# Eight-layer transformer kernel: the first mixture's LayerNorm and turns placed inside the first attention's last tiles, and waits of the feature attention changed

## The reference

```python
x = x + _L0_xattn_ref(_layernorm(x, axis=-1), ctx_2048, ...)   # layer 0: quantized attention, 16 heads
x = x + _L0_ffn_ref(_layernorm(x, axis=-1), ...)               # layer 1: first mixture, shared expert
...
x = x + _L2_ffn_ref(_layernorm(x, axis=-1), ...)               # layer 5: second mixture
x = x + _L3_xattn_ref(_layernorm(x, axis=-1), ctx_2048, ctx_2048)  # layer 6: feature attention
x = x + _L3_ffn_ref(_layernorm(x, axis=-1), ...)               # layer 7: keyed experts and an MLP
```

```python
# layer 0, end of the attention
out = _qdq(o) @ _qdq(wp).T + bp
# layer 1, the router
logits = h.astype(jnp.float32) @ gate_weight.astype(jnp.float32).T
scores = jax.nn.softmax(logits, axis=-1)
topk_w, topk_i = _group_limited_topk(scores)
# layer 5, the weighted sum of two experts a token
for e in range(NUM_EXPERTS):
    gate = jax.nn.silu(jnp.einsum('bsd,dh->bsh', x, W1[e]))
    val = jnp.einsum('bsd,dh->bsh', x, W3[e])
    y = jnp.einsum('bsh,hd->bsd', gate * val, W2[e])
    out = out + combine[..., e:e + 1] * y
# layer 6
qk = jnp.einsum('bdm,bdn->bmn', qh, kh) * scale
sm = jax.nn.softmax(qk, axis=-1)
ret = jnp.einsum('bmn,bcn->bcm', sm, vh)
```

## Time and profile before

| | us |
|---|---|
| median of 3 runs | 1147.91 |
| lowest and highest of them | 1144.64 and 1151.24 |
| the profiled execution | 1144.83 |
| its span, first to last instruction | 1143.1 |
| PE busy in it | 1027.7 (90%) |
| DVE busy in it | 574.1 (50%) |
| ACT, POOL busy in it | 367.9 (32%), 260.5 (23%) |
| mean granted clock of TensorE | 0.946 |

### The profile page before, as it was taken

How to read it: one execution, slowest core, us unless ns; L and a number is a source line. 1 busy time by engine, 2 the same in 40 slices (tenths; PEclk the granted TensorE clock), 3 DMA queues, 4 the chain that set the end, 5 groups by cost and what they waited for, 6 DMA issues and landing times.

```text
span 1143.1 us, 17534 instructions
## 1 busy us (share of the span) xinstructions
PE 1027.7 (90%) x6658; PEld 687.7 (60%) x6658; DVE 574.1 (50%) x1312; ACT 367.9 (32%) x687; POOL 260.5 (23%) x335
## 2 busy tenths in 40 slices
PE   5877999989999999988864899999939999998989
PEld 4665599546767676667654677777713434453467
DVE  7985523444334343445476112212166787647792
ACT  3651233232121212213310222212104666736660
POOL 4221342410000000003521222222142443302350
PEclk9995999999999999999895999999966999989999
DMA  9002033211011010056016112111060000020000
GB/s 290 22 2 101 3 95 93 88 47 28 15 37 35 28 38 5 11 200 255 2 57 256 33 35 102 35 33 37 19 232 1 2 1 1 2 74 1 0 6 33
DMA packets 37433, 67.26 MB, mean 59 GB/s; under 512 B 4456, under 2 KB 27080, under 8 KB 35816
## 3 DMA queue, kind: packets, MB, share of 16 engines
q1 hardware_dynamic: 29960, 51.98, 13.3%
q0 software_dynamic: 4080, 11.15, 3.5%
q10 hardware_dynamic: 3312, 3.02, 0.8%
HBM read 54.72 MB, written 11.40 MB: 58 GB/s over the span
## 4 chain that ended last, share of the span: by engine, by line
PE 73%; DVE 16%; ACT 3%; issue 3%; DMA 3%; POOL 2%; SPq 0%; POOLq 0%; DVEq 0%; ACTq 0%
PE bank L354 20%; PE bank L1192 12%; PE bank L1216 7%; PE bank L1542 5%; PE bank L2244 4%; PE bank L2269 3%; PE bank L2290 3%; PE bank L1552 3%; PE bank L1205 2%; PE bank L1527 2%; PE bank L2726 2%; PE bank L1517 2%; PE bank L2308 1%; DVE big L2519 1%; PE bank L1177 1%
## 5 line engine op out<-in xcount | busy, mean ns | idle before, releaser
L1192 PE MATMUL bank<-big 128*128 x552 | 147.7, 417 | 0.6 <-ACT big L1068 0.6
L354 PE MATMUL bank<-XNT,big 128*128 128x512 f32 x296 | 135.9, 607 | 6.4 <-DVE big L2472 3.8
L1192 PEld LDWEIGHTS bank<-big 128*128 128x128 f32 x552 | 98.2, 191 | 39.4 <-issue 2.6
L270 POOL TENSOR_TENSOR rstd<-ve,half 128x1 f32<-128x1 f32 x56 | 32.7, 588 | 340.1 <-DVE ve L264 339.8
L2244 PE MATMUL bank<-big,xs 32*128 32x512 f32 x256 | 88.1, 736 | 19.4 <-DVE xs L281 18.5
L354 PEld LDWEIGHTS bank<-XNT,big 128*128 128x128 f32 x296 | 54.8, 193 | 69.3 <-issue 59.5
L2111 DVE TENSOR_REDUCE big<-bank 128x2 f32<-128x512 f32 x128 | 81.9, 685 | 24.3 <-PE bank L2244 23.7
L1216 PE MATMUL bank<-big 128*128 (+1 forms) x368 | 87.2, 380 | 1.1 <-ACT big L1083 1.1
L1004 DVE TENSOR_TENSOR big<-big,bank 128x704 f32<-128x704 f32 x23 | 20.5, 889 | 124.7 <-ACT big L1076 124.7
L2190 ACT ACTIVATE big<-bank 128x1024 f32<-128x1024 f32 x64 | 64.9, 1024 | 38.6 <-PE bank L2269 38.3
L354 PE MATMUL bank<-CTXT,big 128*128 128x512 f32 (+1 forms) x192 | 67.0, 493 | 10.9 <-DMA big<-wvT 10.9
(11 more groups left out here) (351 smaller groups left out, 1798.5 us busy)
## 6 DMA issues: line engine op xcount, KB each, us to landing
big<-m_gu SPq DMA_DIRECT2D x8, 1408.0 KB
big<-m_d SPq DMA_DIRECT2D x8, 768.0 KB
big<-a_qk SPq DMA_DIRECT2D x16, 256.0 KB, 3.0
yg<-big ACTq DMA_DIRECT2D x23, 128.0 KB
big<-m_gu SPq DMA_DIRECT2D x8, 352.0 KB
big<-a_o SPq DMA_DIRECT2D x16, 128.0 KB, 2.1
xn<-XNT SPq DMA_DIRECT2D x8, 256.0 KB, 5.9
big<-f_keys SPq DMA_DIRECT2D x1, 2048.0 KB, 9.1
```

Source lines behind the costliest of these rows:

```text
L270: e.tensor_tensor(k.rstd[at % NT][:, :], k.ve[at % NT][:, :], k.half[:, 0:1], ALU.pow).then_inc(k.ln_rstd, 1)
L354: ins = e.matmul(out, a, b, start=start and n == 0, stop=stop and n == len(pairs) - 1)
L1192: ins = e.matmul(out, xgT[s % 2][:, kb, :], WB[:, bass.ds(at[s] + (kb * 2 * F + c * chunk), chunk)], start=kb == 0, stop=kb == KB - 1)
```

## The change

**First mixture.** `experts` lends stage 0 five functions (`stats`, `norm`, `turn`, `logits`, `rows`), and stage 0 issues them among its last steps. DVE makes the statistics of tiles 0 to 3 between `outputs(6)` and `result(6)`, normalises 0 to 2 ahead of `outputs(7)` and 3 behind it, makes the statistics of 4 to 6 ahead of `result(7)`, and the rest behind it; the clears come last. POOL makes its powers for tiles 0 to 3, 4 to 6 and 7 in three instructions in place of eight. PE turns tiles 0 to 2 and makes the logits of 0 and 1 around `out_rows(7)` and `result(7)`; the other turns and logits follow. `XN` moves behind `sg` and `sh` in SBUF, and with it the second attention's `XS`; `TURN` becomes banks 1 and 5, which stage 0 no longer uses by then.

```diff
@@ attention_qdq, dve
+            if front and i == NT - 1:
+                for t in range(4):
+                    front["stats"](e, t)
             if i > 0:
                 result(i - 1)
...
+        if front:
+            for t in range(3):
+                front["norm"](e, t)
         outputs(NT - 1)
+        if front:
+            front["norm"](e, 3)
+            for t in range(4, 7):
+                front["stats"](e, t)
         result(NT - 1)
+        if front:
+            front["stats"](e, 7)
+            for t in range(4, NT):
+                front["norm"](e, t)
@@ attention_qdq, act
+        if front:
+            front["rows"](e, 0)
+            front["rows"](e, 1)
         out_rows(NT - 1)
+        if front:
+            front["rows"](e, 2)
@@ attention_qdq, pe
+        if front:
+            front["turn"](e, 0)
+            front["turn"](e, 1)
+            front["logits"](e, 0)
         out_rows(NT - 1)
+        if front:
+            front["turn"](e, 2)
         result(NT - 1)
+        if front:
+            front["logits"](e, 1)
@@ experts
+    def front_stats(e, t):
+
+        e.wait_ge(k.x_tile, done0 - NT + t + 1)
+        ln_stats_dve(e, k, k.chain(e, "dve"), t, t % 2)
...
+    ahead = 3 if shared_expert and l >= 1 else 0
+    if ahead:
+        k.front[1] = dict(stats=front_stats, norm=norm_x, turn=turn_x, logits=logits, rows=rows_in)
+
+    def pool_first(e):
+        if ahead:
+            ln_rstd_tiles_pool(e, k, at0, 0, 4)
+            ln_rstd_tiles_pool(e, k, at0, 4, 7)
+            ln_rstd_tiles_pool(e, k, at0, 7, 8)
```

```diff
@@ experts, dve
-        for t in range(NT):
+        def combine(t):
...
+        if not shared_expert and k.front.get(6):
+            k.front[6]["combine"] = combine
+            return
+        for t in range(NT):
+            combine(t)
@@ feature_attention
+    if l >= 6:
+        k.front[6] = {}
+    y_ps, y_all = k.moe["y_ps"], k.moe_at["y_ps"]
+
+    def ready(e):
+
+        e.wait_ge(y_ps, y_all)
...
+        def x_of(t):
+
+            if k.front.get(6):
+                k.front[6]["combine"](t)
+                e.wait_ge(k.x_tile, done0 - NT + t + 1)
+
         e.wait_ge(k.masks, masks0 + 2)
+        x_of(0)
         ln_stats_dve(e, k, ch, 0, 0)
+        x_of(1)
         norm(0)
...
+        x_of(2)
+        x_of(3)
         for u in range(NU):
@@ program, run
-                if n > 1 and who != "sp":
-
+                if "ready" in s and who != "sp":
+                    s["ready"](e)
+                elif n > 1 and who != "sp":
                     e.wait_ge(k.x_tile, LOADED + 8 * (n - 1))
```

More of the change, by code:

```diff
@@ L487, in result @@
             e.tensor_tensor(k.X[:, t, :], k.X[:, t, :], k.bank[:, V, D:2 * D], ALU.add).then_inc(k.x_tile, 1)
+        front = k.front.get(1)
         e.wait_ge(k.x_first, 16)
@@ L865, in pool @@
     def pool(e):
-        for t in range(NT):
+        for t in range(0 if ahead else NT):
             ln_rstd_pool(e, k, at0 + t, t % 2)
@@ L910, in dve @@
         ch = k.chain(e, "dve")
-        for t in (0, 1):
-            ln_stats_dve(e, k, ch, t, t)
+        if not ahead:
+            for t in (0, 1):
+                ln_stats_dve(e, k, ch, t, t)
         for n in range(4):
@@ L915, in dve @@
             ch.mark(e.memset(sums[n][:, 0:E], 0.0))
[L916 to L920, removed]
+        for t in range(0 if ahead else NT):
+            norm_x(e, t)
             if t + 2 < NT:
-                ln_stats_dve(e, k, ch, t + 2, p)
+                ln_stats_dve(e, k, ch, t + 2, t % 2)
         lg = k.bank[:, LOGIT, 0:NT * E].rearrange("p (t e) -> p t e", e=E)
@@ L1040, in dve, with rows_in, turn_x, logits @@
                     k.front[2]["norm"](e, n)
-    def act(e):
[L1043 to L1048, removed]
+    def rows_in(e, t):
+        e.wait_ge(k.xt_ps, at0 + t + 1 + CREDIT)
+        dst = k.XNT[:, :, t * P:(t + 1) * P] if shared_expert else k.xT[t % 2][:, :, :]
+        if not shared_expert and t >= 2:
+            after(e, "lg_ps", t - 1)
+        e.copy(dst, k.bank[:, TURN[t % 2], 0:D].rearrange("p (k m) -> p k m", k=KB)).then_inc(k.xt_sb, 1)
+    def turn_x(e, t):
+        e.wait_ge(k.ln_out, at0 + t + 1)
+        e.wait_ge(k.xt_sb, at0 + t + 1)
+        for kb in range(KB):
+            ins = e.transpose(k.bank[:, TURN[t % 2], kb * P:(kb + 1) * P], XN[:, t, kb * P:(kb + 1) * P], k.ident[:, :])
+        ins.then_inc(k.xt_ps, 1)
+    def logits(e, t):
+        if t == 0:
+            after(e, "gate_ld", ends["gate_ld"])
+        e.wait_ge(k.xt_sb, at0 + t + 1 + CREDIT)
+        xT = k.XNT[:, :, t * P:(t + 1) * P] if shared_expert else k.xT[t % 2]
+        tell(mm(e, k.bank[:, LOGIT, t * E:(t + 1) * E], [(xT[:, kb], gw[:, kb]) for kb in range(KB)]), "lg_ps")
+    def front_stats(e, t):
+        e.wait_ge(k.x_tile, done0 - NT + t + 1)
+        ln_stats_dve(e, k, k.chain(e, "dve"), t, t % 2)
+    def norm_x(e, t):
+        e.wait_ge(k.ln_rstd, at0 + t + 1)
+        e.tensor_scalar(XN[:, t], k.X[:, t, :], k.mv[t][:, 0:1], k.rstd[t][:, 0:1], ALU.subtract, ALU.mult)\
+            .then_inc(k.ln_out, 1)
+    ahead = 3 if shared_expert and l >= 1 else 0
[6 more added lines that the diff above has]
+            ln_rstd_tiles_pool(e, k, at0, 7, 8)
+    def act(e):
+        for t in range(ahead, NT):
+            rows_in(e, t)
         def shared(n):
@@ L1128, in shared_down @@
                     [(sh[0:n, t // 4, b, t % 4 * P:(t % 4 + 1) * P], shd[0:n, b]) for b, n in enumerate(FB)]), "shy_ps")
[L1130 to L1133, removed]
[L1134 to L1139 removed]
+        if not ahead:
+            turn_x(e, 0)
+        for t in range(max(ahead - 1, 0), NT):
             if t + 1 < NT:
[L1141 to L1144 removed]
+                turn_x(e, t + 1)
+            logits(e, t)
         if shared_expert:
@@ L2129, in rest @@
             t, n = divmod(u, UNITS)
+            if half == 1 and u < UNITS:
+                x_of(u + 4)
             if n == 0 and half == 0 and t + 2 < NT:
```

23 lines of the change are left out of this document (8 added, 15 removed).

## The result

| | before | after |
|---|---|---|
| median of 20 runs, us | 1149.80 | 1142.34 |
| lowest and highest | 1144.64 and 1152.60 | 1140.11 and 1145.66 |
| ratio, 95% interval | | 0.9935 (0.9925 to 0.9945) |
| the profiled execution's span | 1143.1 | 1143.8 |

The change makes the kernel 7.5 us faster (6.3 to 8.6), where 6.8 were forecast. The two profiled executions do not show it: their spans are alike. The one of before was among the fastest of its kernel, the one of after, 1145.5 us in all, among the slowest of its own. So no gain is read from the spans; every stretch is measured by itself, between two instructions that both kernels have.

The account below looks back on a forecast made before the run. The last-ending chain, 73% PE and 16% DVE, was taken as the bound, with exposed hops at layer 0's end and layer 6's start. Gains 5.4 + 1.4 = 6.8 us off the median 1147.91 gave 1141.1, range 1135 to 1146.

Parts of the forecast that it names:

- Both: Stretch from start of outputs(6) to start of the routing; the first mixture's logits were forecast to end 5.4 us earlier.
- the Score: Time from start of the last instruction of layer 5's sums to layer 6's first score; forecast 1.4 us shorter.
- DVE ahead of outputs(7): End of layer 0: four statistics, a power and three normalisations make outputs(7) 0.6 us late, bounds 0 to 1.1.
- PE: Turns and logits of first tiles fit gaps, projection ends at 96.41, tile 4 just in time, logits end 5.4 us earlier.
- Part 2: Passage to layer 6: statistics directly behind the last sum, power not behind the keys; 1.4 us, bounds 0.7 to 1.6.
- A: Rival: layer 5's sums do get spread out inside layer 6, first score 8.6 us early, 12.5 us gained; 4%.
- B: Rival: DVE's new work delays the last tile more, handed through without slack; gain only 4.9 us, 1143.0; 22%.
- C: Rival: DVE and POOL block one another, nearest at tile 4's normalisation beside a power; up to 0.66 us, 1141.8; 6%.
- D: Rival: layer 6's new start leads to a low TensorE clock for longer, some 20 us more giving 1151; 4%.
- its counterpart: Rival: TensorE's clock in layer 6 rises some 6 us earlier, giving 3 us more, 1138; 6%.
- a rise of the clock more than 5 us behind the logits' end: Sign of a wrong forecast, gain given back; the expected lag was some 3 to 4 us, as before.
- a stretch after 110 that is longer than before by more than 1 us: Sign of a wrong forecast: the gain was made and then given back later in the kernel.

Follow-up runs that it names:

- three_first: Changed kernel with statistics of three tiles instead of four made first on DVE, tile 3's moved behind outputs(7); ratio to the kernel before 0.9940.
- after_third: The changed kernel itself, unmodified, run and profiled a third time beside other kernels on the same chip; ratio to the kernel before 0.9942.
- after_again: The changed kernel itself, unmodified, run once more for a second profile; ratio to the kernel before 0.9938.
- part2_only: Changed kernel without the functions lent to layer 0, so only layer 6's new wait is left; ratio to the kernel before 0.9997.
- part1_again: Same program as part1_only, traced a second time; no timing given, its trace shows 7.52 us from result(7) to the routing.
- part1_only: Changed kernel with layer 6's new wait taken out, so only the first mixture's part is left; ratio to the kernel before 0.9951.
- sums_deferred: Changed kernel with k.front[6] made true, so later tiles' sums come inside layer 6; ratio to the kernel before 0.9890, 12.6 us faster.

## Why the prediction was right

**Where the gain lies.** Both shrank by 5.52 us for 5.4 forecast, the Score by 1.50 for 1.4. Of the total, 7.5 us in the first comparison, and 7.1 and 6.7 in the two others, 7.0 are these two. The clock's rise in the tail, 1.3 us in 3 of 11 traces, adds some tenths that were not forecast. The time forecast, 1141.1, and the 1142.34 measured differ mostly by the kernel before: its median was 1147.91 in the 3 runs that the forecast rests on and 1149.80 in 20.

**DVE ahead of outputs(7).** Forecast 0.6 us late, measured 0.39. The power began 0.30 behind the last `ve` and took 1.03, as forecast. But the statistics began 0.08 ahead of the end of `outputs(6)`, not 0.03 behind it, and each overlapped the one before as in the rows. DVE starts an independent instruction before the last has ended, which I had allowed for in part 2 and not here.

**PE.** The last projection began at once behind turn 2, and from `result(7)` to the routing it took 7.54 us. Forecast were 103.8 for the logits' end, with the projection's end at 96.4: 7.4. The "just in time" of the forecast missed by a little: DVE had normalised tile 4 by 99.01 + 0.41 = 99.42, and PE began its turn at 99.47, 1.30 behind tile 3's turn at 98.17 where a tile costs 1.17. So 0.13 us were lost there. Turn 2 cost nothing, where 0.06 were forecast: from `out_rows(7)` to the projection it took 1.15 us before and after. With 0.21 less delay of DVE, 0.06 less of turn 2 and some 0.14 more in the tail, the forecast's 5.4 becomes the 5.5 measured.

**Part 2.** That the sums are not spread out was read from the order of the instructions, and the trace bears it out: all 16 sums ahead of the statistics. The two halves of its gain came as forecast: the statistics behind the last sum by 0.41 instead of 1.21, the power no longer behind the keys.

**The rivals.** A did not happen, and its price was right when it was made to: 12.6 us for 12.5. Its terms were nearly so: the first score came 8.6 us earlier behind the first sum (3.45 for 12.06), as forecast, and Tile 0 was 2.3 longer than before, where 1.5 were forecast; the trace had the clock's rise in the tail besides. B's mechanism is real, since each us on DVE is handed through, but its price was too high: 0.39 us of delay for the 1.1 of its bound. C cost nothing where the prediction had placed it: the four normalisations from 99.01 on took 1.37 us, with POOL's power at 99.17 beside them; three without any took 1.06, and a fourth at the same distance gives 1.38. A wait shows on POOL's side, though. The power at 99.17 took 0.65 us, as the 655 ns one of the earlier trace rows, also of one tile, did beside normalisations; in `three_first` one of the same form took 0.54 beside statistics alone:

```profile
93.17 0.54 POOL L275 TENSOR_TENSOR rstd<-ve,half 128x1 f32<-128x1 f32 x1 [5.20 <-DVE ve L264]
97.36 0.64 POOL L275 TENSOR_TENSOR rstd<-ve,half 128x1 f32<-128x1 f32 x1 [0.67 <-DVE ve L264]
```

The second of these ran beside normalisations again. The power at 99.17 ended at 99.82, and DVE's normalisation of tile 7, the fourth of its row, was not due before 100.0, so it cost nothing. Further on C's mechanism did act on the chain; that is told under what was off.

D and its counterpart did not show: Tile 0 lies between 45.4 and 46.9 us in all ten traces with the sums in a row, 46.1 before.

**What was off.** The prediction named a rise of the clock more than 5 us behind the logits' end as a sign that it was wrong. It came: the windows show 0.50 at 108 and 0.59 at 110, some 5.6 us behind 105.2. It cost nothing, since from the routing's start to DVE's copy of the counts it took 8.58 us, where it had taken 9.01 before. Before, DVE's chain of small instructions set that stretch, and PE waited 1.10 us for its end; in the changed kernel PE, at 1.2 GHz for longer, finished its matmuls only 0.1 us after it could have gone on. The 0.43 us less come from one instruction of DVE's chain, here of before and then of after, each with POOL's product beside it:

```profile
115.82 1.26 POOL L872 TENSOR_TENSOR big<-big 128x512 f32<-128x512 f32 x1 [9.66 <-ACT big L1056]
116.52 0.62 DVE L734 TENSOR_SCALAR big<-big 128x64 f32<-128x64 f32 x1
```

```profile
112.53 0.20 DVE L764 TENSOR_SCALAR big<-big 128x64 f32<-128x64 f32 x1
112.84 1.26 POOL L903 TENSOR_TENSOR big<-big 128x512 f32<-128x512 f32 x1 [13.02 <-ACT big L1128]
```

Where POOL has begun before it, DVE's instruction ends 0.05 to 0.06 us behind POOL's, in all nine traces in which the two meet (0.42 to 1.12 us); in the four others it takes 0.20. That is rival C's mechanism, on the chain behind the logits, where the prediction had priced no such wait. It can't be put down to the change alone, for the same program had it in one trace and not in another (0.20 in `after` and `after_third`, 0.91 in `after_again`). The sign was a bad one, for it named a cause and not a time.

A second sign came as well: a stretch after 110 that is longer than before by more than 1 us. From the routing to the first sum of layer 5 the trace of before has 725.4 us and that of after 727.5, and the last layer took 139.61 and 142.78. Together with 1.5 us ahead of `outputs(6)`, where the change moved nothing, this is why the spans are alike. But `part2_only`, whose instructions up to layer 6 are in the order of before, has 729.9 for the first of these stretches, and two traces of one program have 142.76 and 138.32 for the second. So these differences occur without the change, and the medians, 7.5 us apart for 7.0 in the two stretches, leave little room for a gain given back. That the spans of two traces say nothing here had no place in the prediction. Two windows of the last layer show where 1.8 of the 3.2 us arise, here of after and then of before, each from 42 us behind the last two reciprocals on:

```profile
1043.00:1053.00 10.00, 9.73 (x16) 4.04 (x16) 5.68 (x9) 4.08 (x7) 0.92 (x1) 0.68 0.01 2
```

```profile
1045.47:1055.47 10.00, 8.09 (x18) 3.32 (x19) 5.67 (x9) 5.17 (x9) 2.56 (x2) 1.00 0.01 2
```

In the one PE's granted clock is 0.68 in the mean and PE is busy almost throughout, in the other it is 1.00 and PE gets more done in less busy time.

## What to carry to other kernels

Where stages meet, look for the engine that idles at the end of one and is the bound at the start of the next: work of the next stage that can run in those gaps is worth its own length plus the idle behind it, and the price is what it puts ahead of the last tile on the other engines, handed through one to one. Read the order of the built program before believing the description of a change: an empty dictionary as a switch had turned off most of this one's second half, worth another 5 us. And compare traces by stretches between two shared instructions, never by their spans, where the kernel's own executions differ by more than the change.

## What the runs showed of the hardware

- One program gave 0.50 or 1.00 as granted clock for PE in the same 2 us (0.50 in `after`, 1.00 in `after_again`; Tail 7.54 and 6.19), and another 138.3 or 142.8 us for its last layer (`part1_again`, `part1_only`).
- DVE and POOL side by side. In `sums_deferred` the first instruction of tile 2's sum took 0.60 us instead of 0.48, beside POOL's spreading of the keys. The Trainium skill, SBUF — State Buffer, section "Who interferes with whom", has a DVE operation with two SBUF inputs and a POOL operation that reads SBUF wait for one another; the direction agrees. The amount is less than a full wait: POOL's operation had 0.32 us still to run (851.50 + 1.89 against 853.07), and DVE's took 0.12 more. The routing's `TENSOR_SCALAR` of 128x64 does show a full one: 0.20 us alone, and up to 1.12 us (`sums_deferred`) beside a POOL operation of 1.26 that began before it. For the normalisation, which by that page can enter a two-port mode, DVE's side showed no wait beside POOL's power (1.37 us for four, where three alone took 1.06); DVE had begun first there, and POOL's power of one tile took 0.65 us, against 0.54 in `three_first` without a normalisation beside it. No row tells in which mode these instructions ran.
- DVE began an independent instruction 0.07 to 0.08 us ahead of the end of the one before it (86.05 against 85.78 + 0.35), so a row of n of them is shorter than n durations.
